# Weighted sums directly behind the scores, pieces of projections behind the sums

## The chip, the cores and the metric

The kernel runs on one core of one Trainium2 chip. The metric is the time of one execution on the device, in microseconds (us); lower is better. Instructions run on five engines that synchronise by semaphores: TensorE (PE, matmuls into PSUM), VectorE (DVE), ScalarE (ACT), GpSimd (POOL), and SyncE (SP), which here issues the DMAs.

## What is computed

One cross-attention block and one quantised linear layer, both with a residual. `x` has 4 batches of 1024 rows, the context 4 batches of 2048 rows, the width is 512, and there are 16 heads of 32 columns.

```python
def xattn(Q, K, V, mask, W_q, W_k, W_v, W_o):
    q = (Q @ W_q.T).reshape(B, -1, NUM_HEADS, D_HEAD).transpose(0, 2, 1, 3)
    k = (K @ W_k.T) ...
    v = (V @ W_v.T) ...
    scores = jnp.einsum('bhqd,bhkd->bhqk', q, k) / np.sqrt(D_HEAD)
    attn = masked_softmax(scores, m)      # exp of clipped scores, divided by its sum
    out = jnp.einsum('bhqk,bhkd->bhqd', attn, v)
    return out.transpose(0, 2, 1, 3).reshape(B, -1, 512) @ W_o.T
...
x = x + xattn(_layernorm(x), ctx_1024, ctx_1024, mask, W_q, W_k, W_v, W_o)
x = x + int8_linear(_layernorm(x), rhs)   # rows and columns scaled to +-127, rounded
```

## The kernel before, in words

The work is a list of segments. Four segments only project (the context of batch 0 to keys and values, its rows to queries). Then come 16 passes, one for each batch and group of four heads; I number them 0 to 15. The last segment finishes the rows of the last batch. A pass has 32 steps (`slot` 0 to 31): two blocks of 512 queries, each against 16 tiles of 128 keys. In step n TensorE does, in the order in which the code is written:

- `scores_of(n, pair)` for two pairs of heads: four matmuls of 128x512 into `scores`. Pair p waits for the exponentials of the same pair of step n-1 (`exp_done`), which free its banks.
- the pieces that the table `BOTH` puts into step n: parts of projections for the next batch or of the output rows of the batch before. `K` and `Q` are 12 matmuls of 128x256 (a key or query tile), `V` and `O` are thirds of a tile (4 matmuls of 128x512), `X` and `T` are transposes, `N` sums squares, `F` is the int8 linear layer of 128 rows. All go through the two banks of `tile`, and each piece waits until the tile two before it has been read out.
- `sums_of(n - LAG, pair)` with LAG 2: the weighted sums, `wsum` += values x exponentials of step n-2, eight matmul records on groups of 32 columns. In steps 1 and 17, where a block of queries is complete, the column sums of `acc` follow (`dsum`, line 769). In the passes 12 to 15 key tiles 3 and 8 are not added up in `acc` but go straight into `dsum` (line 763), in steps 5, 10, 21 and 26.

ScalarE takes the exponentials of step n (`probs`, line 918), then reads out the pieces of step n (`stage_hi`, line 946, and its squares into `v_stage`, line 950; `row_hi`; `v_stage`; `qT`), and in steps 1 and 17, behind these, copies `dsum` and `wsum` out:

```python
ct.wait(act, "acc_summed", k)
...
nc.scalar.copy(denoms[:, :], dsum[:, :]).then_inc(sems["denoms_copied"], 1)
ct.wait(act, "o_stored", 32 * (k - 1))
nc.scalar.copy(sums[:, :], wsum[:, :]).then_inc(sems["sums_copied"], 1)
```

The first `sums_of` of the next block (step 2 or 18) waits for `sums_copied`, since it writes `wsum` from the start. VectorE adds the exponentials up in `acc` (two adds a step, line 1142); between the two it does the second half of reading out `K`, `Q` and `N`; the work of the other pieces it does at the start of the following step. `probs` is a ring of four steps. The division goes through memory: `denoms` is stored to `den_c` (step 2 or 18), VectorE takes the reciprocal in step 4 or 20 (line 1147), and it comes back as `denoms`. SyncE issues all transfers in the order of its code, each behind its own waits.

Pieces that the prediction speaks of: step 17 holds `K11` (second key tile of the second half) in the passes 0 to 11; step 13 holds `F0` and a third of `O1` in the passes 4 to 15, and `O1` waits there for `row_lo` (line 1095) of step 12; step 10 holds the transpose `T0`, which waits for `q8`, quantised by VectorE (lines 1073 to 1078) and ScalarE (line 935). Step 23 holds `Q3`, step 26 the work `bound` (`safe`, line 1064), for whose result SyncE waits.

Of the kernel before, what the change touches and what calls it, by code (L numbers as in the profile page):

```python
# [40 lines left out]
LAG = 2  # L41
# [169 lines left out]
def program(nc, x, ctxT, mask, wqT, wkT, wvT, woT, rhsT, out):  # L211
    es = ExitStack()
    with es:
# [479 lines left out]
        def _(pe):  # L693
# [14 lines left out]
            def body(seg, ct, it):  # L708
# [25 lines left out]
                def scores_of(n, pair):  # L734

                    qb, kt = divmod(n, KT)
                    if pair == 0 and kt == 0:
                        ct.wait(pe, f"q_loaded{qb}", 64)
                    if pair == 0 and qb == 0 and kt % 4 == 0:
                        ct.wait(pe, f"k_loaded{kt // 4}", 64)  # L740
                    ct.wait(pe, "exp_done", 2 * n + pair - 1)
                    for h in (2 * pair, 2 * pair + 1):
                        last = nc.tensor.matmul(scores[:, h, :], k_stack[:, kt // 4, h, (kt % 4) * P:(kt % 4 + 1) * P],  # L743
                                                q_stack[:, qb, h, :], start=True, stop=True)
                    last.then_inc(sems["scores_full"], 1)

                def sums_of(n, pair):

                    qb, kt = divmod(n % STEPS, KT)
                    if pair == 0 and kt == 0:  # L750
                        ct.wait(pe, "sums_copied", 2 * (n // STEPS) + qb)
                    if pair == 0 and qb == 0 and kt % 4 == 0:
                        ct.wait(pe, f"v_loaded{kt // 4}", 16)
                    ct.wait(pe, "exp_done", 2 * n + pair + 1)
                    ct.wait(pe, "probs_ready", 2 * n + pair + 1)
                    for h in (2 * pair, 2 * pair + 1):
                        last = nc.tensor.matmul(wsum[DH * h:DH * h + DH, :], v_sb[:, kt, DH * h:DH * h + DH],  # L757
                                                probs[:, n % RING, h, :], start=(kt == 0), stop=(kt == KT - 1))
                    if pair == 0:
                        return  # L760
                    if kt in seg.direct:
                        for h in range(G):
                            last = nc.tensor.matmul(dsum[DH * h:DH * h + DH, :], ones[:, :], probs[:, n % RING, h, :],
                                                    start=(kt == seg.direct[0]), stop=False)
                    last.then_inc(sems["step_summed"], 1)
                    if kt == KT - 1:
                        ct.wait(pe, "add_done", 2 * seg.adds * (2 * (n // STEPS) + qb + 1))
                        for h in range(G):
                            last = nc.tensor.matmul(dsum[DH * h:DH * h + DH, :], ones[:, :], acc[:, h, :],  # L769
                                                    start=not (seg.direct_before if n < 0 else seg.direct), stop=True)  # L770
                        last.then_inc(sems["acc_summed"], 1)

                for slot in range(STEPS):

                    summing = seg.prev and slot < LAG or seg.b and slot >= LAG
                    for pair in range(2):
                        if seg.b:
                            scores_of(slot, pair)
                    for p in seg.pieces(slot):
                        kind = p[0]  # L780
                        opening = kind not in "VO" or p[-1] == 0
# [61 lines left out]
                                                        start=(kc == 0), stop=(kc == KC - 1))  # L843
                        if full:
                            last.then_inc(sems["tile_full"], 1)
                    if summing:
                        for pair in range(2):
                            sums_of(slot - LAG, pair)

            def between(ct):  # L850
                if ct.s == FIRST_B:
# [21 lines left out]
                pe.wait_ge(w_done, 4)  # L873

            runs(pe, body, between)
            last_rows_tensor(pe, three_passes)

# [368 lines left out]
```

## Time and profile before

| | |
|---|---|
| median of 3 runs | 1937.39 us (1935.2 to 1943.0) |
| the profiled execution | 1937.39 us, span 1935.6 us, granted TensorE clock 0.982 on average |
| TensorE (PE) | 1815.8 us busy, 94% of the span |
| weight loads (PEld) | 995.7 us, 51% |
| VectorE (DVE) | 1533.6 us, 79% |
| ScalarE (ACT) | 1296.8 us, 67% |
| GpSimd (POOL) | 284.2 us, 15% |
| DMA | 276.36 MB, mean 143 GB/s |

The profiled execution is the median run itself; 1.8 us of it lie outside the span. Matmuls are pipelined, so a row of TensorE overlaps the next: how long a block holds the engine is read from the start of one block to the start of the next, not from the duration of a row.

### The profile page before, as it was taken

What the parts mean: (1) busy time and instruction counts of PE and PEld (TensorE: products, weight loads), DVE (VectorE), ACT (ScalarE), POOL (GpSimd) and SP (SyncE); (2) the same over time, 40 slices, a digit from 0 to 9 for tenths busy, and PEclk for the clock granted to TensorE, in tenths of its full rate; (3) what the DMA queues carried; (4) which work ended last, traced back from release to release, by engine and by line L of the source; (5) the groups of instructions that cost most, each with busy time, mean ns of one, the idle gap of its engine ahead of it and who ended that gap; (6) DMA issues with size and microseconds to landing.
All of it is one profiled execution on the core that took longest, in us unless ns stands there. A gap on an engine that the chain in (4) does not pass through costs nothing.

```text
span 1935.6 us, 31331 instructions
## 1 busy us (share of the span) xinstructions
PE 1815.8 (94%) x10584; PEld 995.7 (51%) x10584; DVE 1533.6 (79%) x1857; ACT 1296.8 (67%) x1682; POOL 284.2 (15%) x200
## 2 busy tenths in 40 slices
PE   5887999999998999999999999999999999999986
PEld 4775555555554555655555565555556333333333
DVE  4335789888886989888898988889898788878875
ACT  3334777777776676776767677677767676767752
POOL 0000011111110212111111211112121112111123
PEclk9998999999998999999999999999999999999997
DMA  6458264645556364665736456473645544546232
GB/s 217 142 177 229 78 158 126 172 121 149 142 153 160 103 171 117 159 165 147 187 102 172 121 144 178 136 192 101 178 116 134 151 128 102 153 103 154 61 115 98
DMA packets 224933, 276.36 MB, mean 143 GB/s; under 512 B 27520, under 2 KB 142208, under 8 KB 224128
## 3 DMA queue, kind: packets, MB, share of 16 engines
q1 hardware_dynamic: 224768, 274.28, 52.7%
q8 instruction: 89, 1.46, 0.3%
q14 instruction: 76, 0.62, 0.1%
HBM read 181.41 MB, written 92.54 MB: 142 GB/s over the span
## 4 chain that ended last, share of the span: by engine, by line
PE 63%; issue 11%; DVE 10%; DMA 8%; ACT 4%; SPq 3%; POOL 2%; DVEq 0%; POOLq 0%; ACTq 0%
PE tile L705 21%; PE scores L743 19%; PE wsum L757 17%; DVE acc L1142 5%; ACT probs L918 2%; DMA den_c<-denoms 2%; PE dsum L769 1%; DMA v_parts<-v_stage 1%; DMA row_lo<-o_parts 1%; DMA denoms<-recip_row 1%; SPq L528 1%; PE tile L837 1%; POOL normed L1199 1%; DMA k_parts<-stage_hi 1%; SPq L540 1%
## 5 line engine op out<-in xcount | busy, mean ns | idle before, releaser
L918 ACT ACTIVATE probs<-scores 128x1024 f32<-128x1024 f32 x1024 | 993.6, 1024 | 377.8 <-PE scores L743 375.0
L1142 DVE TENSOR_TENSOR acc<-acc,probs 128x1024 f32<-128x1024 f32 x864 | 1085.0, 1294 | 87.1 <-ACT probs L918 85.4
L743 PE MATMUL scores<-q_stack,k_stack 128*128 128x512 f32 x2048 | 634.9, 429 | 8.6 <-ACT probs L918 6.3
L743 PEld LDWEIGHTS scores<-q_stack,k_stack 128*128 128x128 f32 x2048 | 339.9, 190 | 512.0 <-ACT probs L918 333.9
L757 PE MATMUL wsum<-probs,v_sb 128*32 128x512 f32 x4096 | 549.5, 608 | 0.5
L1186 POOL TENSOR_TENSOR rstd<-var_eps,minus_half 128x1 f32<-128x1 f32 x56 | 53.2, 951 | 834.4 <-DVE var_eps L1044 834.4
L757 PEld LDWEIGHTS wsum<-probs,v_sb 128*32 128x32 f32 x4096 | 81.7, 108 | 152.7 <-issue 74.5
L1142 DVE TENSOR_TENSOR acc<-probs 128x1024 f32<-128x1024 f32 x64 | 76.5, 1221 | 99.5 <-PE dsum L769 97.8
L705 PE MATMUL tile<-ctx_hi,wk_hi 128*128 128x256 f32 x448 | 127.8, 285 | 21.0 <-DVE wk_lo L998 17.9
L705 PE MATMUL tile<-ctx_hi,wk_lo 128*128 128x256 f32 x448 | 126.9, 283 | 0.0
L705 PE MATMUL tile<-ctx_lo,wk_hi 128*128 128x256 f32 x448 | 126.3, 282 | 0.0
L1172 POOL TENSOR_TENSOR o_hi<-sums,denoms 128x512 fp32r<-128x512 f32 x32 | 54.0, 1687 | 430.9 <-DMA denoms<-recip_row 430.9
L1199 POOL TENSOR_TENSOR normed<-normed,xr 128x512 f32<-128x512 f32 x24 | 53.1, 2212 | 340.2 <-DVE normed L1115 340.2
L705 PEld LDWEIGHTS tile<-ctx_hi,wk_hi 128*128 128x128 f32 x448 | 84.9, 190 | 26.8 <-issue 17.9
L705 PE MATMUL tile<-wv_hi,ctx_hi 128*128 128x512 f32 x224 | 94.4, 422 | 3.2 <-DVE row_lo L1095 3.2
L705 PE MATMUL tile<-wv_hi,ctx_lo 128*128 128x512 f32 x224 | 89.7, 400 | 0.0
L705 PE MATMUL tile<-wv_lo,ctx_hi 128*128 128x512 f32 x224 | 89.5, 400 | 0.0
L705 PEld LDWEIGHTS tile<-ctx_hi,wk_lo 128*128 128x128 f32 x448 | 85.5, 191 | 4.4
L705 PEld LDWEIGHTS tile<-ctx_lo,wk_hi 128*128 128x128 f32 x448 | 85.3, 190 | 0.0
L946 ACT CAST stage_hi<-tile 128x256 fp32r<-128x256 f32 x144 | 54.1, 376 | 33.5 <-issue 17.1
L1088 DVE TENSOR_TENSOR q_stack<-tile,q_stack 128x256 fp32r<-128x256 f32 x48 | 20.4, 425 | 67.6 <-ACT q_stack L946 67.6
L705 PE MATMUL tile<-row_hi,wq_hi 128*128 128x256 f32 x256 | 73.5, 287 | 0.0
(153 smaller groups left out, 1807.9 us busy)
## 6 DMA issues: line engine op xcount, KB each, us to landing
k_stack<-k_parts SPq DMA_DIRECT2D x256, 256.0 KB, 5.8
q_stack<-q_parts SPq DMA_DIRECT2D x128, 256.0 KB, 7.1
v_parts<-v_stage SPq DMA_DIRECT2D x64, 256.0 KB, 3.2
v_sb<-v_parts SPq DMA_DIRECT2D x64, 256.0 KB, 5.2
raw<-ctxT SPq DMA_DIRECT2D x28, 512.0 KB, 5.8
k_parts<-stage_hi SPq DMA_DIRECT2D x96, 128.0 KB, 3.3
k_parts<-stage_lo SPq DMA_DIRECT2D x96, 128.0 KB, 3.3
k_parts<-q_stack SPq DMA_DIRECT2D x64, 128.0 KB, 3.7
```

The costliest lines, as they stand in the source:

```text
L528: sp.dma_start(k_stack[at:at + DH, quarter, :, :].bitcast(F32), src[:, part].rearrange("o (h d) t -> d (o h) t", d=DH)).then_inc(sems[f"k_ ...
L540: sp.dma_start(q_stack[DH * r:DH * r + DH, qb, :, :].bitcast(F32), src[:, r // 2].rearrange("o (h d) t -> d (o h) t", d=DH)).then_inc(sems ...
L705: last = nc.tensor.matmul(dst, s(kc), m(kc), start=(n == 0), stop=(n == len(todo) - 1))
L743: last = nc.tensor.matmul(scores[:, h, :], k_stack[:, kt // 4, h, (kt % 4) * P:(kt % 4 + 1) * P], q_stack[:, qb, h, :], start=True, stop=True)
L757: last = nc.tensor.matmul(wsum[DH * h:DH * h + DH, :], v_sb[:, kt, DH * h:DH * h + DH], probs[:, n % RING, h, :], start=(kt == 0), stop=(k ...
L918: nc.scalar.activation(probs[:, slot % RING, 2 * pair:2 * pair + 2, :], scores[:, 2 * pair:2 * pair + 2, :], ACT.Exp, scale=1.0 / math.sqr ...
L946: nc.scalar.copy(to, tile[:, bank, 0:ROWS]).then_inc(sems["hi_done"], 1)
L1088: nc.vector.tensor_tensor(to, tile[:, bank, 0:ROWS], staged_hi.bitcast(F32), ALU.subtract) \
L1142: nc.vector.tensor_tensor(acc[:, heads, :], other, now, ALU.add).then_inc(sems["add_done"], 1)
L1172: nc.gpsimd.tensor_tensor(o_hi[:, :], sums[:, :], denoms[:, :], ALU.mult).then_inc(sems["attn_normed"], 1)
L1186: nc.gpsimd.tensor_tensor(rstd[:, u:u + 1], var_eps[:, u:u + 1], minus_half[:, :], ALU.pow).then_inc(sems["rstd_ready"], 1)
L1199: nc.gpsimd.tensor_tensor(normed[:, :], normed[:, :], xr[:, :], ALU.add).then_inc(sems["y_added"], 1)
```

## The change

In every step the two calls of `sums_of` move from behind the pieces to ahead of them. Nothing is added or removed, and the other engines' code is the same.

```diff
                     for pair in range(2):
                         if seg.b:
                             scores_of(slot, pair)
+                    if summing:
+                        for pair in range(2):
+                            sums_of(slot - LAG, pair)
                     for p in seg.pieces(slot):
                         kind = p[0]
...
                         if full:
                             last.then_inc(sems["tile_full"], 1)
-                    if summing:
-                        for pair in range(2):
-                            sums_of(slot - LAG, pair)
```

The first place is on TensorE around the end of step 17 of pass 0 (passes 0 to 11 are alike there). Before, with the end of `K11` first:

```order
L705 MATMUL tile<-ctx_hi,wk_hi 128x256
L705 MATMUL tile<-ctx_hi,wk_lo 128x256
L705 MATMUL tile<-ctx_lo,wk_hi 128x256
L757 MATMUL wsum<-probs,v_sb 32x512 x4
L769 MATMUL dsum<-acc,ones 32x512 x4
L743 MATMUL scores<-q_stack,k_stack 128x512 x4
```

The same place now, from the sums of step 17 to the sums of step 18:

```order
L743 MATMUL scores<-q_stack,k_stack 128x512 x4
L757 MATMUL wsum<-probs,v_sb 32x512 x4
L769 MATMUL dsum<-acc,ones 32x512 x4
L705 MATMUL tile<-ctx_hi,wk_hi 128x256
...
L705 MATMUL tile<-ctx_lo,wk_hi 128x256
L743 MATMUL scores<-q_stack,k_stack 128x512 x4
L757 MATMUL wsum<-probs,v_sb 32x512 x4
```

`wsum` and `dsum` of step 17 stand ahead of the twelve matmuls of `K11`, and only the scores of step 18 lie between `K11` and the first sums of the next block; before, `K12` and `X1` lay there too.

The second place is on TensorE in step 10 of pass 12 (passes 13 to 15 are alike), with the transpose `T0`. Before:

```order
L743 MATMUL scores<-q_stack,k_stack 128x512 x4
L830 MATMUL tile<-ident_bf,q8 128x128 x4
L757 MATMUL wsum<-probs,v_sb 32x512 x4
L763 MATMUL dsum<-probs,ones 32x512 x4
L743 MATMUL scores<-q_stack,k_stack 128x512 x4
```

Now:

```order
L743 MATMUL scores<-q_stack,k_stack 128x512 x4
L757 MATMUL wsum<-probs,v_sb 32x512 x4
L763 MATMUL dsum<-probs,ones 32x512 x4
L833 MATMUL tile<-ident_bf,q8 128x128 x4
L743 MATMUL scores<-q_stack,k_stack 128x512 x4
```

The transposes stand behind both blocks of sums and directly ahead of the next scores.

## Rows read from the trace of the kernel before

**Rows 1.** Timeline, TensorE, pass 7: start, us, engine, line, operation [idle before <-releaser].

```profile
1000.42 1.20 PE L743 MATMUL scores<-q_stack,k_stack 128*128 128x512 f32 x4
...
1003.98 1.20 PE L743 MATMUL scores<-q_stack,k_stack 128*128 128x512 f32 x4
...
1006.33 0.28 PE L705 MATMUL tile<-ctx_lo,wk_hi 128*128 128x256 f32 x1
1006.54 1.07 PE L757 MATMUL wsum<-probs,v_sb 128*32 128x512 f32 x8
1007.42 1.04 PE L769 MATMUL dsum<-acc,ones 128*32 128x512 f32 x8
1008.39 1.19 PE L743 MATMUL scores<-q_stack,k_stack 128*128 128x512 f32 x4
```

**Rows 2.** Timeline, ScalarE, steps 17 and 18 of pass 7.

```profile
1006.64 0.37 ACT L946 CAST stage_hi<-tile 128x256 fp32r<-128x256 f32 x1
1007.11 0.42 ACT L950 ACTIVATE v_stage<-stage_hi 128x256 bf16<-128x256 f32 x1
1008.53 0.59 ACT L971 COPY denoms<-dsum 128x512 f32<-128x512 f32 x1 [1.00 <-PE dsum L769]
1009.01 0.59 ACT L973 COPY sums<-wsum 128x512 f32<-128x512 f32 x1
...
1011.80 0.42 ACT L950 ACTIVATE v_stage<-stage_hi 128x256 bf16<-128x256 f32 x1
1012.13 0.57 ACT L956 CAST row_hi<-tile 128x512 fp32r<-128x512 f32 x1
```

**Rows 3.** Timeline, VectorE, steps 6 to 13 of pass 6.

```profile
852.39 0.25 DVE L1147 RECIPROCAL recip_c<-den_c 128x16 f32<-128x16 f32 x1 [3.32 <-DMA den_c<-denoms]
...
878.86 0.68 DVE L1095 TENSOR_TENSOR row_lo<-tile,row_hi 128x512 fp32r<-128x512 f32 x1
```

**Rows 4.** Timeline, TensorE, step 13 of pass 6: first matmul of O1, next scores.

```profile
879.59 0.50 PE L705 MATMUL tile<-wo_hi,row_hi 128*128 128x512 f32 x1 [2.51 <-DVE row_lo L1095]
...
881.70 1.21 PE L743 MATMUL scores<-q_stack,k_stack 128*128 128x512 f32 x4
```

**Rows 5.** Waits: engine, line, waited for: us in total, times, longest us.

```profile
PEld tile L705 <- DVE row_lo L1095: 25.7, 12, 3.2
...
PE tile L830 <- ACT q L935: 14.4, 4, 4.6
```

**Rows 6.** Timeline, VectorE, pass 9: second half of Q3, and `safe`.

```profile
1259.10 0.42 DVE L1088 TENSOR_TENSOR stage_lo<-tile,stage_hi 128x256 fp32r<-128x256 f32 x1
...
1271.92 0.20 DVE L1064 TENSOR_SCALAR safe<-norms 16x1 f32<-16x1 f32 x1
```

**Rows 7.** Waits of SyncE's queue.

```profile
SPq L197 <- DVE safe L1064: 120.8, 16, 11.0
...
SPq L197 <- DMA v_parts<-v_stage: 45.5, 11, 6.1
```

**Rows 8.** Timeline, TensorE, step 10 of pass 12.

```profile
1541.74 0.59 PE L830 MATMUL tile<-ident_bf,q 128*128 128x128 bf16 x4 [4.58 <-ACT q L935]
...
1545.83 1.96 PE L743 MATMUL scores<-q_stack,k_stack 128*128 128x512 f32 x4
```

**Rows 9.** Timeline, ScalarE, step 10 of pass 12.

```profile
1541.50 1.92 ACT L918 ACTIVATE probs<-scores 128x1024 f32<-128x1024 f32 x2
```

**Rows 10.** Timeline, TensorE, step 10 of pass 13.

```profile
1631.53 0.38 PE L830 MATMUL tile<-ident_bf,q 128*128 128x128 bf16 x4 [2.66 <-ACT q L935]
1631.85 1.06 PE L757 MATMUL wsum<-probs,v_sb 128*32 128x512 f32 x8
...
1634.48 2.01 PE L743 MATMUL scores<-q_stack,k_stack 128*128 128x512 f32 x4
```

**Rows 11.** Timeline, ScalarE, step 10 of pass 13.

```profile
1631.30 1.92 ACT L918 ACTIVATE probs<-scores 128x1024 f32<-128x1024 f32 x2
```

**Rows 12.** Busy time by stretch; the number ahead of the last two is the clock.

```profile
1632.90:1636.30 3.40, 3.40 (x14) 1.17 (x4) 3.40 (x4) 1.35 (x3) 0.00 (x0) 0.50 0.38 141
...
875.00:881.70 6.70, 4.19 (x24) 1.81 (x21) 6.70 (x7) 3.05 (x4) 0.00 (x0) 1.00 0.40 115
```

## The prediction

> **What bounds the kernel now.** I read the page first. TensorE is busy for 94% of the span, far ahead of VectorE with 79% (the table above), so the question is whether TensorE's queue gets shorter or only another order. I then laid the timeline of TensorE out by steps. A step with a key or query piece goes from scores to scores in 3.56 us, 1000.42 to 1003.98, with no idle time in it [rows 1]; the reader is to see that the engine passes from block to block. Most steps of the passes 0 to 11 are like that, and for them the order of the blocks within the step cannot matter: the same matmuls follow each other. So I looked for the steps that are longer than their matmuls, and asked of each what the piece or the sums wait for. Three places carry the argument.
>
> First, step 13 of the passes 4 to 11: `O1` waits for `row_lo`, 2.51 us in pass 6 [rows 4]; in the table of waits this releaser stands with 25.7 us in 12 waits [rows 5]. VectorE had been behind since step 6, where it waited 3.32 us for `den_c` to land and then worked without a pause up to `row_lo`, 26.47 us later, 852.39 to 878.86 [rows 3]. So the start of `O1` hangs on the landing of `den_c`, and on nothing that TensorE does in between.
>
> Second, step 10 of the passes 12 to 15: `T0` waits for `q`, 14.4 us in four waits, the longest 4.6 [rows 5]. It again comes at the end of VectorE's work behind the reciprocal.
>
> Third, a place with no wait now: step 18. ScalarE copies `wsum` out at 1009.01, done at 1009.60 [rows 2], while TensorE is in the scores that began at 1008.39 [rows 1]; the sums that need it come only behind `K12` and `X1`.
>
> **The change part by part.** It moves matmuls within one queue, 16 passes of 32 steps, and neither removes nor adds any. A step without a wait keeps its length. Two things shift: sums come a piece earlier (0.9 to 1.5 us), and pieces come 1.0 us later, the time for which the sums hold the engine (a block of the same eight records, `dsum`, holds it for 0.97, 1007.42 to 1008.39 [rows 1]).
>
> *Step 17, a new wait.* Step 17 lasts 4.41 us, 1003.98 to 1008.39. Now `K11` ends the step instead of ending 2.35 us into it (its last matmul starts at 1006.33 [rows 1]). That last matmul will start about 0.12 us ahead of the next scores, so at 4.29. ScalarE's cast follows the last matmul's start by 0.31 (1006.33 to 1006.64), the square follows the cast by 0.47 (1006.64 to 1007.11), the next readout follows a square by 0.33 (1011.80 to 1012.13), and the copy of `wsum` follows the copy of `dsum` by 0.48 and takes 0.59 [rows 2]. All of these stand ahead of `sums_copied` in ScalarE's queue: 4.29 + 0.31 + 0.47 + 0.33 + 0.48 + 0.59 = 6.47 us after the start of step 17, or 2.06 into step 18. The sums of step 18 now stand directly behind the scores and would start 1.12 into the step (1.03 for the scores and 0.09 for the turn to the narrow groups, which is what the 0.21 from the last matmul of `K11` to the sums shows against a spacing of 0.12 [rows 1]). With 0.04 for the signal they start at 2.10. The new wait is 0.98 us. Queued behind it are `K12`, `X1` and the scores of step 19; nothing follows in the steps 18 to 29 that is waiting for another engine anyway, so TensorE does not get it back. It occurs where `K11` stands in step 17, in 12 passes: +11.8 us. Bounds: 0, if ScalarE gets through in time; 1.3 us each (15.6) if a copy also waits for VectorE or a transfer.
> Step 1 has no such cost: its piece is a third of `O0`, of which ScalarE reads nothing out, so the copies come earlier there.
>
> *Step 13, passes 5 to 11.* The start of `O1` stays bound to VectorE. Before, a third of `O1` and the sums followed, 2.11 us (879.59 to 881.70 [rows 4]); now the sums are done before the wait, so 1.0 us less. But the landing of `den_c` moves. `den_c` goes out behind a burst of loads which SyncE starts when `v_parts` has been stored (45.5 us of waiting, 11 times), and that store goes out behind a chain that starts with `safe` (SyncE waits 120.8 us for it, 16 times [rows 7]). `safe` comes 12.82 us after the second half of `Q3` on VectorE, 1259.10 to 1271.92 [rows 6], without a pause between them, and that half of `Q3` follows the piece, which is now 1.0 to 1.1 us later. So `den_c`, the reciprocal and `O1` come 1.1 us later. Per pass 1.1 - 1.0 = +0.1, over seven passes +0.7 us. Bounds: -1.0 each (-7) if the transfers absorb the delay, +1.1 each (+7.7) if the sums' place brings nothing. Waits that appear between step 6 and step 13 cost nothing as long as they end before `O1` may start: that wait is their cover, 2.5 us a pass.
>
> *Step 10, passes 12 to 15.* `T0` starts when `q` is ready. Before, sums, `dsum` and the half-rate clock followed: 2.95 us from `T0` to the next scores in pass 13 (1631.53 to 1634.48 [rows 10]) and 4.09 in pass 12 (1541.74 to 1545.83 [rows 8]). Now the scores of step 11 follow `T0` (0.32 to the next block in pass 13 [rows 10]) and wait only for the first exponential of step 10, which ends about 1.0 after 1631.30 [rows 11], or 1541.50 [rows 9]: at 1632.3 and 1542.5. Saved: 2.2 and 3.3 us. With the mean, 2.75, for the four passes: -11.0. In pass 12 the later `safe` of pass 11 takes 1.1 back; the passes 13 to 15 have no `safe` ahead of them. Together -9.9 us. Bounds: -13.2, and -1.0 each (-4) if ScalarE, with two exponentials of 0.96 us a step still queued, holds the next steps back.
>
> Sum against the profiled execution: 1937.39 + 11.8 + 0.7 - 9.9 = 1940.0 us. That execution is also the median of the runs shown, so nothing is corrected.
>
> **The rivals.** About 0.5%, 9.7 us, is what a measurement of this kernel can tell from no change.
>
> *A, the forecast:* new wait in step 18, gain at `T0`, step 13 even: 1940, own range 1933 to 1947. Chance 0.55.
>
> *B, the gain at `T0` is given back (slower).* After `T0` the steps 11 and 12 have no piece and ScalarE's queue is full: two exponentials of step 10 to 1633.2, the copy `qT`, then two more of step 11 [rows 11]. If ScalarE and then VectorE (which is behind there) set the pace, the steps 11 and 12 stretch by what step 10 saved. Then 1937.4 + 11.8 + 0.7 = 1950. It decides at a gain below 2.8 us of the 9.9. For it speaks that both engines are busier in plain steps; against it that their backlog is a matter of two steps, and steps 13 to 15 are bound by TensorE again. Chance 0.18.
>
> *C, the delay of `safe` does not reach `den_c`.* The burst then starts as before, and each of the passes 5 to 12 gains 1.1 us more: 1940.0 - 8.8 = 1931. For it speaks that transfers wait on each other in several places; against it the 120.8 us for which SyncE waits for `safe` [rows 7]. Chance 0.12; with other waits shorter as well it ends below 1928.
>
> *D, the clock.* In pass 13 the granted clock was 0.50 for 3.4 us after the 2.66 us of idle time at `T0`, while 2.51 us of idle time in pass 6 left it at 1.00 [rows 12]. If each of the 12 new waits of 1 us brought such a stretch, up to 1.7 us each would be added, 1940 + 20 = 1960. The shorter idle time in front speaks against it. Chance 0.04.
> The Trainium skill, "TensorE: Matmul & The Clock Gate", section "Why this matters for your kernels", advises to keep idle gaps between bursts of matmuls short, since idle stretches return the array to half rate. [...] The trace agrees at `T0` (half rate behind 2.66 us) and disagrees in pass 6 (full rate through 2.51 us) [rows 12], so the measurement keeps the chance low.
>
> *E, the order does not matter anywhere:* ScalarE's copies are quicker than I reckon and the later pieces cost what the earlier sums bring, 1937. Chance 0.11.
>
> **How the numbers follow.** The likeliest case gives 1940. The range takes in C and B: 1928 to 1952; D and the far end of C stay outside. Faster by over 0.5%, below 1927.7: part of C and E, 0.10. Slower, above 1947.1: B and D and the tail of A, 0.25. Within: 0.65.
>
> **What would show it.** In the trace after: a wait of TensorE in step 18 for `sums` (line 973) of about 1 us, 12 times; without it the first term is wrong. `T0` followed by scores in under 1.2 us, with step 11 no longer than before; if steps 11 and 12 grow, rival B holds. The wait for `row_lo` still there, with `den_c` landing 1 us later counted from the start of the pass; if it lands as before, C. The dsum of step 1 should come 0.9 us earlier and change nothing. The prediction is wrong as a whole if a wait appears that no row here shows, for instance for `squared` or `lo_done` in the key steps, since every piece is read out 1 us later in 32 steps of each pass.

## The result and the profile after

The changed kernel takes 1949.59 us, median of 6 runs (1948.75 to 1954.38), against 1937.16 us for the kernel before, median of 6 runs. The ratio is 1.006 with a 95% interval of 1.0037 to 1.0083: 12 us slower. The forecast was 1940, range 1928 to 1952; the direction and the range hold, the likeliest case was too low by 10 us. Of all runs in this document one, in the experiment e2, was in the slow state (2454.85 us at a granted clock of 0.65); it is left out of every median and ratio.

The page of the changed kernel, span and TensorE:

```profile
span 1946.9 us, 31331 instructions
...
PE 1804.3 (93%) x10584; PEld 985.8 (51%) x10584; DVE 1522.9 (78%) x1857; ACT 1286.9 (66%) x1682; POOL 315.3 (16%) x200
```

Of the engines only GpSimd is busy for longer than before (315.3 us against 284.2).

Timeline of TensorE, steps 17 and 18 of pass 7, the place of [rows 1]:

```profile
1013.58 1.10 PE L743 MATMUL scores<-q_stack,k_stack 128*128 128x512 f32 x4
1014.61 1.07 PE L757 MATMUL wsum<-probs,v_sb 128*32 128x512 f32 x8
1015.49 1.04 PE L769 MATMUL dsum<-acc,ones 128*32 128x512 f32 x8
...
1017.88 0.29 PE L705 MATMUL tile<-ctx_lo,wk_hi 128*128 128x256 f32 x1
1018.00 1.08 PE L743 MATMUL scores<-q_stack,k_stack 128*128 128x512 f32 x4
1020.09 1.16 PE L757 MATMUL wsum<-probs,v_sb 128*32 128x512 f32 x8 [1.01 <-ACT sums L973]
```

And ScalarE there, the place of [rows 2]:

```profile
1018.20 0.37 ACT L946 CAST stage_hi<-tile 128x256 fp32r<-128x256 f32 x1 [1.71 <-PE tile L705]
1018.66 0.42 ACT L950 ACTIVATE v_stage<-stage_hi 128x256 bf16<-128x256 f32 x1
1018.99 0.57 ACT L971 COPY denoms<-dsum 128x512 f32<-128x512 f32 x1
1019.45 0.59 ACT L973 COPY sums<-wsum 128x512 f32<-128x512 f32 x1
```

The reader is to see that `dsum` was written by 1016.5, and that its copy stands idle behind the readout of `K11` until 1018.99. The copy of `wsum` ends at 1020.04 and the sums start at 1020.09, 2.09 us into step 18.

Five lines of the table of waits:

```profile
DVE xr L1103 <- DMA xr<-x: 42.2, 10, 4.9
ACT v_stage L961 <- DMA v_parts<-v_stage: 30.4, 14, 4.3
PEld wsum L757 <- ACT sums L973: 20.7, 19, 1.4
...
PE wsum L757 <- ACT sums L973: 12.0, 12, 1.0
PE tile L833 <- ACT q L935: 9.8, 4, 3.2
```

Twelve waits for `sums` on TensorE are the predicted ones. ScalarE's wait for the stores of `v_parts` (7.1 us in 6 waits before) and VectorE's wait for `xr` (3.9 us in 3) are not in the prediction.

To see where the time went I took the length of each step from the start of its scores to the start of the next in both timelines, and summed the differences over the passes. The span grew by 11.3 us:

| steps | us | |
|---|---|---|
| 18, passes 0 to 11 | +13.1 | predicted, +11.8 |
| 30 and 31, passes 0 to 11 | +11.1 | not predicted |
| 17 and 19 | +4.2 | not predicted |
| 20 | +2.3 | +0.9 to +1.1 in passes 4, 6, 8 and 10, -0.3 in passes 0 to 3, 7 and 9 |
| 24 | -3.6 | not predicted, a gain |
| 0 to 13, passes 5 to 11 | -2.8 | predicted +0.7 |
| 10 to 12, passes 12 to 15 | -5.0 | predicted -9.9 |
| the rest | -8.0 | steps 0 to 13 of pass 4 (-3.3), other small gains, +2 outside the steps |

### The profile page after: what moved, and what is told of

The parts are those of the page before. It is cut to its first block, busy times and chain, and to the rows that moved or that the text cites. A ratio compares the mean times of both kernels' runs of the same rounds, so it can differ in the third digit from the quotient of the medians.

```text
span 1946.9 us, 31331 instructions
## 1 busy us (share of the span) xinstructions
PE 1804.3 (93%) x10584; PEld 985.8 (51%) x10584; DVE 1522.9 (78%) x1857; ACT 1286.9 (66%) x1682; POOL 315.3 (16%) x200
## 4 chain that ended last, share of the span: by engine, by line
PE 43%; issue 17%; DMA 14%; DVE 13%; ACT 5%; SPq 4%; POOL 4%; DVEq 0%; ACTq 0%; POOLq 0%
PE tile L705 18%; PE wsum L757 11%; PE scores L743 10%; DVE acc L1142 8%; DMA den_c<-denoms 3%; DMA v_parts<-v_stage 3%; POOL normed L1199 3%; ACT probs L918 3%; DMA row_lo<-o_parts 1%; DMA o_parts<-sums 1%; DMA xr<-x 1%; SPq L528 1%; SPq L540 1%; DMA denoms<-recip_row 1%; PE dsum L769 1%
## 5 line engine op out<-in xcount | busy, mean ns | idle before, releaser
L1142 DVE TENSOR_TENSOR acc<-acc,probs 128x1024 f32<-128x1024 f32 x864 | 1073.8, 1288 | 37.1 <-ACT probs L918 34.9
L743 PE MATMUL scores<-q_stack,k_stack 128*128 128x512 f32 x2048 | 600.4, 410 | 22.9 <-ACT probs L918 19.6
L743 PEld LDWEIGHTS scores<-q_stack,k_stack 128*128 128x128 f32 x2048 | 357.2, 190 | 233.7 <-ACT probs L918 148.1
L705 PE MATMUL tile<-ctx_hi,wk_hi 128*128 128x256 f32 x448 | 137.4, 307 | 23.4 <-DVE wk_lo L998 17.8
L1199 POOL TENSOR_TENSOR normed<-normed,xr 128x512 f32<-128x512 f32 x24 | 87.2, 3633 | 333.2 <-DVE normed L1115 333.2
L1088 DVE TENSOR_TENSOR stage_lo<-tile,stage_hi 128x256 fp32r<-128x256 f32 x144 | 60.9, 423 | 83.2 <-ACT stage_hi L946 77.3
L705 PE MATMUL tile<-wv_hi,ctx_lo 128*128 128x512 f32 x224 | 95.8, 428 | 0.0
L705 PE MATMUL tile<-wv_lo,ctx_hi 128*128 128x512 f32 x224 | 95.6, 427 | 0.0
L961 ACT COPY v_stage<-tile 128x512 f32<-128x512 f32 x64 | 37.5, 586 | 84.3 <-PE tile L705 52.8
```

The lines of the kernel that those rows point to most:

```text
L705: last = nc.tensor.matmul(dst, s(kc), m(kc), start=(n == 0), stop=(n == len(todo) - 1))
L961: nc.scalar.copy(v_stage[:, :], tile[:, bank, :]).then_inc(sems["v_copied"], 1)
L1088: nc.vector.tensor_tensor(to, tile[:, bank, 0:ROWS], staged_hi.bitcast(F32), ALU.subtract) \
L1142: nc.vector.tensor_tensor(acc[:, heads, :], other, now, ALU.add).then_inc(sems["add_done"], 1)
L1199: nc.gpsimd.tensor_tensor(normed[:, :], normed[:, :], xr[:, :], ALU.add).then_inc(sems["y_added"], 1)
```

## The experiments

All are edits of the condition under which a step has the new order, of ScalarE's order, or both. "New" is sums ahead of pieces. Ratios are to the kernel before, taken on the same chip, with a 95% interval; its median there was 1937.82 us for e1 to e4, 1939.21 for e5 to e8 and 1937.15 for e9 to e11. Runs of one kernel scatter by up to 14 us around their median, so the ratios carry the verdicts on the whole, and the steps of the profiled executions those on places. Only one execution of each kernel was profiled; in e2, e5 and e8 it is the fastest one, 6, 9 and 14 us below the median.

**e1: ScalarE's copies first.** The changed kernel, with the block on `slot == first + 1` moved ahead of the loop over the pieces.

```diff
+                    for first, k, on in ((0, 0, seg.prev), (KT, 1, seg.b)):
+                        if on and slot == first + 1:
+                            ct.wait(act, "acc_summed", k)
...
                     for p in seg.at(slot):
                         kind = p[0]
...
-                    for first, k, on in ((0, 0, seg.prev), (KT, 1, seg.b)):
-                        if on and slot == first + 1:
-                            ct.wait(act, "acc_summed", k)
```

> The changed kernel, with ScalarE's copies of dsum and wsum in steps 1 and 17 moved ahead of the readout of that step's piece. Theory: step 18 lasts 5.08 us instead of 3.99 because these copies stand behind the readout of K11; with the copies first they are done about 4.1 us into step 17, the wait in step 18 goes, and 12 x 1.09 = 13.1 us come back: about 1936.5. Rival: the wait is only moved, since K11 is then read out 0 to 1 us later and the exponentials of step 18 stay late: 1947 to 1950, with steps 18 and 19 longer together than 8.0 us.

Measured: 1946.1 us, ratio 1.0037 (1.0019 to 1.0055). The wait is gone: step 18 lasts 3.9 us instead of 5.08, 14 us less over the 12 passes, and of `wsum` waiting for `sums` only this is left:

```profile
PEld wsum L757 <- ACT sums L927: 3.5, 7, 0.5
```

That is what it was in the kernel before. But the median fell by 3.5 us only, and the interval overlaps that of the changed kernel (1.0037 to 1.0083), so this gain is not told from none; it is short of the 14 us. In the profiled execution step 20 grew by another 5.5 us over the passes 4 to 11, step 7 by 2.8 there, and the steps 10 to 12 of the passes 12 to 15 gave back 4.9, while the steps 30 and 31 lost 5.3. The cause of the wait was the one I named; its removal was mostly taken up elsewhere.

**e2 and e3: the old order in one step.** The changed kernel, with the old order in step 23 (`Q3`) alone, and in step 29 (the last third of a value tile) alone.

```diff
-                    if summing:
+                    if summing and slot not in (23,):
...
+                    if summing and slot in (23,):
+                        for pair in range(2):
+                            sums_of(slot - LAG, pair)
```

> The changed kernel with the old order (piece Q3 ahead of the sums) in step 23 alone. Theory S: steps 30 and 31 became 9.4 us longer in the passes 4 to 11 because Q3 is read out 1 us later, safe with it, the stores of v_parts behind it, and ScalarE's readout of the last value tile in step 30 waits for such a store; with safe back in its place most of it returns, and the landing of den_c and row_lo come 1 us earlier as well (up to 7.7 us in step 13): 1933 to 1941. Rival V: the value tile itself, which now ends step 29, is what is late; then steps 30 and 31 stay and the time is 1947 to 1950.

> The changed kernel with the old order (last third of the value tile ahead of the sums) in step 29 alone. Theory S (the store behind safe is late): no gain, 1948 to 1951, steps 30 and 31 as in the changed kernel. Rival V (the readout of the tile is late because the tile ends the step): steps 30 and 31 lose up to 9.4 us in the passes 4 to 11: about 1940.

Measured: e2 1942.18 us, ratio 1.002 (1.0003 to 1.0037); e3 1951.49 us, 1.005 (1.0028 to 1.0073). With the old order in step 23 the growth of steps 30 and 31 over the passes 0 to 11 is 2.2 us instead of 11.1; with the old order in step 29 it is 9.4. So what is late is the chain behind `safe`, not the value tile itself. The growth is uneven: 5.8 of the 11.1 us are in the passes 6 and 8. The row that carries it is ScalarE in step 30 of pass 6, in the changed kernel:

```profile
946.86 0.58 ACT L961 COPY v_stage<-tile 128x512 f32<-128x512 f32 x1 [3.18 <-DMA v_parts<-v_stage]
947.34 1.95 ACT L918 ACTIVATE probs<-scores 128x1024 f32<-128x1024 f32 x2
```

and in the kernel before:

```profile
937.89 0.59 ACT L961 COPY v_stage<-tile 128x512 f32<-128x512 f32 x1 [0.58 <-DMA v_parts<-v_stage]
938.43 1.94 ACT L918 ACTIVATE probs<-scores 128x1024 f32<-128x1024 f32 x2
```

The store before it has not landed, `v_stage` cannot be overwritten, and both exponentials of step 30 stand behind the copy: they start 3.2 us into the step instead of 0.8. SyncE issued that store at 941.48, 2.6 us ahead of the step's scores, where it had been 3.8 (933.86): 1.2 us later. The copy then started 5.4 us behind the issue instead of 4.0, so about half of the delay is a transfer that took longer; why, is not shown.

**e4: the old order in step 13** (`F0` and a third of `O1`), otherwise the changed kernel; the edit is that of e2 with 13 for 23.

> The changed kernel with the old order (F0 and a third of O1 ahead of the sums) in step 13 alone. Theory G: GpSimd's residual add of F0 lasts 5.6 us instead of 2.2 in the passes 4, 6, 8 and 10 because VectorE reaches its adds 1 us later there and leaves it no gap; xr is then loaded late, VectorE waits for it in step 17, the stores of the key tiles are late and step 20 is 1.4 us longer. With the old order step 13 grows by 1.0 us in 8 passes (+8), and steps 17, 19 and 20 give back 3.0 + 6 us: 1945 to 1950, the add at 2.2 us again. Rival: the add is slow for another reason (its place in the pass shifts with everything else); then steps 17 and 20 stay long and the time is 1955 to 1959.

Measured: 1957.81 us, ratio 1.0099 (1.0075 to 1.0122). Both halves have to be read. The chain came out: GpSimd's adds take 2.0 us on average instead of 3.6,

```profile
L1202 POOL TENSOR_TENSOR normed<-normed,xr 128x512 f32<-128x512 f32 x24 | 49.2, 2048 | 332.1 <-DVE normed L1118 332.1
```

VectorE waits for `xr` once, for 0.4 us, step 17 is back to its 4.41 us, and step 20 lasts 3.95 or 3.96 us in every one of the passes 4 to 11, 6.2 us less in all. But step 13 grew by 14.0 us over the changed kernel, not 8. The cause is TensorE's clock behind the wait for `row_lo`. In pass 6 of e4:

```profile
883.87 0.79 PE L705 MATMUL tile<-wo_hi,row_hi 128*128 128x512 f32 x1 [3.16 <-DVE row_lo L1098]
...
885.87 1.65 PE L757 MATMUL wsum<-probs,v_sb 128*32 128x512 f32 x8
887.45 1.20 PE L743 MATMUL scores<-q_stack,k_stack 128*128 128x512 f32 x4
```

From `O1` to the next scores it is 3.58 us, where [rows 4] have 2.11, and the granted clock (the number ahead of the last two) was 0.50 for 3.4 us of it:

```profile
883.70:887.10 3.40, 3.23 (x12) 1.36 (x12) 3.40 (x4) 0.00 (x0) 0.00 (x0) 0.50 0.02 5
```

This is so in five of the eight passes (2.83 to 3.69 us, 6.6 us more than 2.12 each time), in the kernel before in pass 8 alone (2.68), and in the changed kernel in none. The length of the wait alone does not decide it: in e4 the clock fell behind waits of 2.65 to 3.16 us and stayed at 1.00 behind 2.65 and 2.91 in the passes 5 and 7, and in the kernel before it fell behind 2.00 and stayed behind 2.74.

**e5, e6, e8: the new order in some steps only,** in the kernel before: in 7, 12, 20, 24 and 27 (e5), in 10 (e6), in all six (e8).

```diff
+                    if summing and slot in (7, 10, 12, 20, 24, 27,):
+                        for pair in range(2):
+                            sums_of(slot - LAG, pair)
                     for p in seg.pieces(slot):
...
-                    if summing:
+                    if summing and slot not in (7, 10, 12, 20, 24, 27,):
```

> The kernel before with the new order in the steps 7, 12, 20, 24 and 27 alone, those with the pieces N, X and T but for step 10. Theory: these steps need less time on TensorE in the new order, 0.3 us for one with N (3.76 to 3.46 in step 24), 0.1 for one with X or T, for no wait; over the passes 0 to 11 that is 13.9 us, of which the wait for row_lo in step 13 swallows 3.4 in the passes 4 to 11: about 1927. Rival: the saving belongs to the neighbours' order as well, or is taken up by waits that shift, and the time is 1934 to 1940.

> The kernel before with the new order in step 10 alone. Theory of the prediction: in the passes 12 to 15 T0 no longer holds the sums back, 2.2 to 3.3 us a pass, 9.9 to 11 us in all: 1927. Rival B: steps 11 and 12 stretch and give back a third to all of it, as in the changed kernel, where step 10 lost 8.4 us and steps 11 and 12 grew by 3.4: 1932 if it is that, 1937 if all is given back.

> The kernel before with the new order in the steps 7, 10, 12, 20, 24 and 27, those with N, X and T. If the gains add, 10 us of the shorter turns and 5 to 10 of step 10: 1917 to 1923, faster than before. If VectorE's chain in the passes 4 to 11 or ScalarE in the passes 12 to 15 takes them up: 1928 to 1937.

Measured: e5 1937.42 us, ratio 0.9987 (0.997 to 1.0004), not told from no change; e6 1934.46 us, 0.9972 (0.9955 to 0.999); e8 1929.06 us, 0.996 (0.9942 to 0.9978), faster than both kernels by 0.4% and more. In e5 the steps 20, 21, 24 and 25 are 7.9 us shorter over the passes 0 to 11 (with 7, 8, 12, 27 and 28 it is 12.8, where 13.9 were expected), but the steps 0 to 13 of the passes 5 to 11 became 6.2 us longer, 4.1 of it in step 13, where the clock was at half rate behind the wait in two passes; the expectation that only 3.4 would be swallowed was too good. In e6 step 10 of the passes 12 to 15 lost 10.9 us and steps 11 and 12 took 4.1 back, 6.8 net, while the steps 0 to 13 of the passes 5 to 11 grew by 3.7, of which 3.0 are again the clock in step 13, in three passes; in e8 the three steps together lost 9.5. The profiled execution of e8 took 1915.4 us; the median is the number to use.

**e7: copies first, and the old order in step 23.**

> The changed kernel with ScalarE's copies first (as in the experiment with the copies alone) and the old order in step 23. If the two costs are independent, 14 us of step 18 and 9 us of steps 30 and 31 come back, 1927. If the first is given back in step 20, where the store of a key tile is late behind the load of xr, as it was with the copies alone (5.5 us in step 20 and 4 in step 7), about 1936 to 1940.

Measured: 1938.79 us, ratio 0.9998 (0.9982 to 1.0014). The second case: the two costs gone, the kernel is only level with the one before. Step 18 lost 14.0 us, and step 20 is 7.5 us longer over the passes 4 to 11 than in the changed kernel; GpSimd's add, told of below, takes 5.60 us in all eight of them.

**e9 and e10: one cost alone.** The kernel before with the new order in steps 17 and 18 only, and in step 23 only.

> The kernel before with the new order in the steps 17 and 18 alone: the one place of the predicted wait by itself. Theory: step 18 waits for the copy of wsum, 1.09 us in each of 12 passes, and nothing covers it: 13 us slower, 1950 to 1952. Rival: what the changed kernel lost elsewhere stands behind this wait too, so that taken alone it costs under 5 us: 1939 to 1944.

> The kernel before with the new order in step 23 alone (Q3 read out 1 us later, safe behind it). Theory S: safe is 1 us late, the stores of v_parts and den_c with it; steps 30 and 31 grow by 5 to 10 us over the passes, and step 13 by 1 us in each of the passes 5 to 11: 1944 to 1954. Rival: it needs the other pieces' delay too, and the time is that of before, 1936 to 1941.

Measured: e9 1953.07 us, ratio 1.0083 (1.0064 to 1.0101); e10 1948.84 us, 1.0055 (1.0036 to 1.0074). Waits of e9:

```profile
PEld wsum L757 <- ACT sums L976: 20.8, 19, 1.4
...
PE wsum L757 <- ACT sums L976: 12.0, 12, 1.0
```

These are the waits of the changed kernel, and step 18 grew by the same 13.1 us, with nothing to cover it. The steps 0 to 13 of the passes 5 to 11 grew by 3.0 in it, all of that through the clock in step 13. In e10 the steps 30 and 31 grew by 0.7 us only, against my expectation of 5 to 10, the steps 23 and 24 by 2.4, and the steps 0 to 13 of the passes 5 to 11 by 6.5, where 7 were expected. The last agreement proves little: 2.3 of the 6.5 are the clock in step 13, and the 4.2 by which `row_lo` is later come back as 3.8 in e5, which leaves step 23 alone. So the new order in step 23 costs 0.55% by itself, but that it does so through `den_c` is not shown, and for the steps 30 and 31 it needs the other shifts of the changed kernel too.

**e11: copies first, and the old order in step 13.**

> The changed kernel with ScalarE's copies first and the old order in step 13. Theory G: with the copies alone 5.5 us came back as a longer step 20, because GpSimd's add of F0 is slow, xr late and the stores of key tiles behind it; with step 13 in the old order the add takes 2.2 us, so step 20 stays at its 3.95 us (31.6 us over the passes 4 to 11), step 18 at 3.92, and against the same kernel without the copies first (1957.8) the full 14 us show: 1944. Rival: step 20 is long for another reason and stays at 5 us in several passes: 1949 to 1952.

Measured: 1945.66 us, ratio 1.0041 (1.0028 to 1.0053). Step 20 is 3.95 to 3.97 us in all passes 4 to 11, step 18 is 3.9, and the ratio is 0.6% below that of e4, where the 14 us of step 18 would be 0.7%. So the part of step 20 that swallowed the gain in e1 goes with GpSimd's slow add. In the whole nothing is won over e1 (1.0037), since the price of the old order in step 13 stands in its place.

## Why the prediction was right or wrong

*The number: inside the range, in part by luck.* The three places of the sum gave 13.1 - 2.8 - 5.0 = +5.3 us instead of +2.6. The other 6.0 of the 11.3 us are what is left of 17.6 of costs (steps 17, 19, 20, 30 and 31) and 11.6 of gains, none of which was in the sum. By the sign that the prediction itself gave, a wait that none of its rows shows, its account of the whole is wrong: VectorE's wait for `xr` grew to 42.2 us.

*The new wait in step 18: right.* Predicted 0.98 us in 12 passes, 11.8 in all; measured 1.09 and 13.1. The sums start at 2.09 us of the step, where I had 2.10. What I mis-sized is when they would have started: the step before the change of order was 3.99 us, and 5.08 - 3.99 is the price; the turns between the blocks around the wait make up the rest. e1 shows the cause (the copies stand behind the readout of `K11`), e9 its price alone.

*Step 13: both terms mis-sized, and their sum has the other sign.* I had +1.1 for the delay of `den_c` and -1.0 for the sums, +0.7 in seven passes; the steps 0 to 13 lost 2.8 us. Counted from the start of the pass, the reciprocal starts 0.60 us later on average of the passes 5 to 11 and `row_lo` ends 0.76 later, 5.3 in all. From `O1` to the next scores it is 1.04 us instead of 2.12, 8.1 less in all, of which 0.6 is the stretch at half rate that pass 8 had before. 5.3 - 8.1 = -2.8. The clock behind this wait was in none of my terms, and it is what made e4 costly: `row_lo` is no later there (0.64 us) than in the changed kernel.

*`T0`: a term mis-sized by a factor of two.* Predicted -9.9, measured -5.0. Pass 13 of the changed kernel, TensorE, in step 10 (before: [rows 10]):

```profile
1648.23 0.38 PE L833 MATMUL tile<-ident_bf,q 128*128 128x128 bf16 x4 [2.28 <-ACT q L935]
1649.05 0.74 PE L743 MATMUL scores<-q_stack,k_stack 128*128 128x512 f32 x2 [0.44 <-ACT probs L918]
```

0.82 us from `T0` to the scores instead of 2.95, and 0.82 in the other three passes as well: 11.15 us less in all, where I had 11.0. So the saving at the spot is there. But `T0` itself starts 2.8 us later in its steps (the steps 0 to 9 ahead of it had become 2.1 us shorter), so that step 10 lost 8.4, and 3.4 of that went back in steps 11 and 12, which is rival B, to a third. The term lies between the two ends that I had named (-4 and -13.2). With fewer other changes the term is larger: 6.8 us in e6 and 9.5 in e8.

*What the prediction had wrong: "nothing follows in the steps 18 to 29 that is waiting for another engine anyway", and the sum made from three places.* I followed the later pieces to `safe`, to `v_parts` and to `den_c`, and stopped there. Two chains lie beside it.

First, the same store of `v_parts` has another customer, ScalarE's readout of the next value tile in step 30, ahead of the exponentials. It waited already in the kernel before, 0.58 us in pass 6 and in five of the 12 passes in all, so the chain had little slack or none: +11.1 us, of which e2 takes 8.9 back.

Second, in steps 14 to 20 of the changed kernel. GpSimd adds the residual of `F0`, while VectorE adds exponentials. In the kernel before VectorE reached the first of these adds 0.03 us after its exponential was done; now it reaches it 1.21 us after, and four are ready. GpSimd in pass 6, before and then after:

```profile
883.67 2.23 POOL L1199 TENSOR_TENSOR normed<-normed,xr 128x512 f32<-128x512 f32 x1 [10.37 <-DVE normed L1115]
```

```profile
889.10 5.60 POOL L1199 TENSOR_TENSOR normed<-normed,xr 128x512 f32<-128x512 f32 x1 [10.37 <-DVE normed L1115]
```

VectorE in the same stretch, before:

```profile
883.54 5.73 DVE L1142 TENSOR_TENSOR acc<-acc,probs 128x1024 f32<-128x1024 f32 x4
```

and after:

```profile
888.94 4.61 DVE L1142 TENSOR_TENSOR acc<-acc,probs 128x1024 f32<-128x1024 f32 x4
893.48 0.14 DVE L1099 COPY mask_cur<-mask_f 128x1 f32<-128x1 f32 x1
898.13 0.75 DVE L1103 SCALAR_TENSOR_TENSOR xr<-tile,mask_cur,xr 128x512 f32<-128x512 f32 x1 [4.51 <-DMA xr<-x]
```

Before, the second of the four took 2.31 us instead of 1.21, and GpSimd's add ended beside it. After, all four took 1.21 us, and GpSimd's add ended only 1.2 us after the last of them. It took 5.60 us in seven of the passes 4 to 11, where it had been 1.3 to 2.2; step 20 is late in four of these seven (in e1 in all seven that have the long add, and not in the one where it took 2.31). `xr` can be loaded only when that result has been stored away, VectorE waits 4.51 us for it with the readout of a key tile queued behind, and the stores of the key tiles are late in SyncE's queue. In step 20, ScalarE waits before the cast of a key tile, by the code (`hi_stored`) for the store of the stage buffer that it overwrites:

```profile
911.49 0.37 ACT L946 CAST stage_hi<-tile 128x256 fp32r<-128x256 f32 x1 [2.90 <-issue]
```

The Trainium skill, "GPSIMD Engine Reference", section "1. Specifications", says that GpSimd shares its SBUF interfaces with VectorE and contends with VectorE instructions that have two SBUF inputs. These adds have two, and this trace agrees: either one add of VectorE is held (2.31 us instead of 1.21) or GpSimd's is (5.60 instead of 2.23). e4 and e11 show the chain: with the old order in step 13 the add is short, and in e4 step 17 is 3.0 us and step 20 6.2 us shorter over the passes than in the changed kernel. That it is the shared interface and not something else in VectorE's order was not tried apart, and why the slow add makes step 20 late in some passes only is open.

*A gain that I priced at nothing.* "A step without a wait keeps its length" is wrong for steps with `N`. TensorE in step 24 of pass 9, before:

```profile
1259.59 1.20 PE L743 MATMUL scores<-q_stack,k_stack 128*128 128x512 f32 x4
1260.72 0.60 PE L837 MATMUL tile<-v_stage,head_sum 128*16 128x256 bf16 x4
1261.25 0.50 PE L705 MATMUL tile<-wv_hi,ctx_hi 128*128 128x512 f32 x1
...
1262.37 1.07 PE L757 MATMUL wsum<-probs,v_sb 128*32 128x512 f32 x8
1263.37 0.98 PE L743 MATMUL scores<-q_stack,k_stack 128*128 128x512 f32 x3
```

and after:

```profile
1272.38 1.09 PE L743 MATMUL scores<-q_stack,k_stack 128*128 128x512 f32 x4
1273.40 1.07 PE L757 MATMUL wsum<-probs,v_sb 128*32 128x512 f32 x8
1274.28 0.60 PE L840 MATMUL tile<-v_stage,head_sum 128*16 128x256 bf16 x4
1274.81 0.50 PE L705 MATMUL tile<-wv_hi,ctx_hi 128*128 128x512 f32 x1
...
1275.84 1.08 PE L743 MATMUL scores<-q_stack,k_stack 128*128 128x512 f32 x4
```

3.78 us became 3.46: the sums pass on to the narrow `N` after 0.88 us instead of 1.00 to the scores, scores follow the value piece after 1.03 instead of the sums after 1.12, and the scores hold the engine for 1.02 instead of 1.13. No wait is involved. e5 measures it: 7.9 us in four steps, while the steps 0 to 13 of the passes 5 to 11 grew by 6.2. In the time it is not shown: e8, which has it, stands at 0.996 and e6, which has not, at 0.9972, with overlapping intervals.

*The rivals.* B was right in kind, to a third. C is not settled: the store of `v_parts` is 1.2 us later in pass 6, but the reciprocal only 0.60 on average, and with step 23 back in the old order (e2) it is still 0.44 later, so how much of this comes through `safe` stays open. D was wrong for the place it named: no stretch at half rate lies in a step 18 behind the 12 new waits of 1.01 us, and the mean clock went from 0.982 to 0.983. The clock counted elsewhere, in steps 10 and 13. The chance of 0.25 for slower by over 0.5% was too small, since I had counted one cost and two gains and given the costs that I could not see no weight.

## What to carry to other kernels

When a block moves within one engine's queue, list every result that now comes later and follow each to all who wait for it, transfers and the reuse of its buffer included; one that already has a short wait has no slack to give. Moving the order only where it pays (six steps of 32, e8) was faster by 0.4% (step 10 alone, e6, by 0.3%), where the same order in every step was slower by 0.6%. Taking one new wait away need not bring its price back: e1 took 14 us out of step 18, and its median was 3.5 us lower. And when a step behind a wait takes longer than its matmuls, look at the granted clock before looking for a late engine: in e4 that was 6.6 us.

## What was not expected of the hardware

GpSimd's add of 128x512 took 1.3 to 5.6 us in one and the same program, 5.6 us where four adds of VectorE ran beside it at 1.21 us each; why VectorE's add is held in one case and GpSimd's in the other, no run here settles. Its median went from 2.2 to 3.3 us. GpSimd's 24 adds in the changed kernel, with durations in ns as least, median and greatest:

```profile
L1199 POOL TENSOR_TENSOR normed<-normed,xr x24: 1277/3328/5606, 658.2 to 1878.3; 128x512 f32<-128x512 f32 x24
```

and of the kernel before:

```profile
L1199 POOL TENSOR_TENSOR normed<-normed,xr x24: 1285/2218/3342, 657.5 to 1868.2; 128x512 f32<-128x512 f32 x24
```

A step of the same matmuls took 3.78 or 3.46 us by the order of its blocks alone. And TensorE's granted clock fell to 0.50 behind a wait of 2.00 us (before, pass 8) and stayed at 1.00 behind one of 2.91 (e4, pass 7).
